# GpSimd's inverse square roots: a power in place of a seed and three Newton steps, in a two-layer decoder on one Trainium2 core

## The reference, cut to what matters

```
x = x + xattn0(layernorm(x), ctx, mask)   # 16 query heads, 8 key heads of 128
x = x + ffn0(layernorm(x))                # silu(gate) * up, weights rounded to float8
x = x + xattn1(layernorm(x), ctx)         # 16 heads of 128, q and k root-mean-square normalised
x = x + moe(layernorm(x))                 # 16 experts, the best 2 for each row
```

```
def _layernorm(x, axis=-1, eps=1e-05):
    return (x - mean(x)) / sqrt(var(x) + eps)

def rmsnorm(x, g, eps=1e-5):
    return x * rsqrt(mean(square(x)) + eps) * g
```

## Time and profile before

| | us |
|---|---|
| three runs, median | 2196.19 |
| three runs, lowest and highest | 2195.21, 2196.66 |
| the profiled execution, span | 2195.1 |
| TensorE busy | 2071.1 |
| VectorE busy | 1566.6 |
| ScalarE busy | 1253.3 |
| GpSimd busy | 574.9 |

### The profile page before, as it was taken

One profiled execution on the slowest core, in us unless ns is written; L12 is line 12 of the kernel. 1 busy time (PEld: TensorE's weight loads), 2 busy tenths in 40 slices (PEclk: granted clock), 3 DMA queues, 4 the chain that ended last, 5 costly groups with the idle time before them and its releaser, 6 DMA issues. The chain is left out here.

```text
span 2195.1 us, 36404 instructions
## 1 busy us (share of the span) xinstructions
PE 2071.1 (94%) x11594; PEld 1788.0 (81%) x11594; DVE 1566.6 (71%) x3714; ACT 1253.3 (57%) x3253; POOL 574.9 (26%) x1480
## 2 busy tenths in 40 slices
PE   5999999999999899999899999999999999599992
PEld 5888988888888778887788888888888887378882
DVE  6787677777779884444677777777777777767775
ACT  4555445455445533324776766677676666567771
POOL 2001001001001002223333434433343433145541
PEclk8999999999999999999999999999999999799996
DMA  7232122121211220002111111111111111278886
GB/s 249 82 99 89 63 85 92 62 89 63 90 63 49 73 77 1 1 1 77 49 58 49 62 63 57 48 57 48 57 62 72 48 40 39 87 269 290 290 275 257
DMA packets 78509, 202.10 MB, mean 92 GB/s; under 512 B 8689, under 2 KB 38409, under 8 KB 66209
## 3 DMA queue, kind: packets, MB, share of 16 engines
q1 hardware_dynamic: 68672, 179.37, 23.5%
q0 software_dynamic: 7520, 16.80, 2.2%
q10 hardware_dynamic: 2176, 4.19, 0.5%
HBM read 179.09 MB, written 29.10 MB: 95 GB/s over the span
## 5 line engine op out<-in xcount | busy, mean ns | idle before, releaser
L733 PE MATMUL bank<-l_wkv_hi,l_ctxT 128*128 128x512 f32 (+1 forms) x768 | 224.8, 364 | 9.0 <-PEq L79 6.9
L1245 DVE TENSOR_TENSOR l_pT_lo<-bank,l_pT_hi 128x512 fp32r<-128x512 f32 x256 | 175.2, 684 | 69.7 <-ACT l_pT_hi L1071 69.6
L1065 ACT ACTIVATE l_probs<-l_scored,l_nbias 128x256 f32<-128x256 f32 x256 | 128.4, 504 | 167.8 <-DVE l_nbias L1318 167.8
L733 PE MATMUL bank<-xnT_hi,l_wq_hi 128*128 128x512 f32 x512 | 208.7, 408 | 0.8 <-DVEq L1551 0.7
L733 PE MATMUL bank<-l_wo_hi,l_oT_hi 128*128 128x512 f32 x512 | 208.4, 407 | 0.7 <-DVE l_oT_lo L1245 0.7
L733 PE MATMUL bank<-l_wo_hi,l_oT_lo 128*128 128x512 f32 x512 | 200.6, 392 | 0.0
L733 PE MATMUL bank<-xnT_hi,l_wq_lo 128*128 128x512 f32 x512 | 200.3, 391 | 0.0
L733 PE MATMUL bank<-l_wo_lo,l_oT_hi 128*128 128x512 f32 x512 | 200.2, 391 | 0.0
L733 PE MATMUL bank<-xnT_lo,l_wq_hi 128*128 128x512 f32 x512 | 200.2, 391 | 0.0
L1071 ACT CAST l_pT_hi<-bank 128x512 fp32r<-128x512 f32 x256 | 150.8, 589 | 67.6 <-PE bank L832 67.6
L1333 DVE TENSOR_SCALAR l_probs<-l_probs,l_rden 128x256 f32<-128x256 f32 x512 | 181.3, 396 | 9.0
(11 more groups left out here) (305 smaller groups left out, 5738.0 us busy)
## 6 DMA issues: line engine op xcount, KB each, us to landing
l_ctxT<-ctx_split SPq DMA_DIRECT2D x63, 1024.0 KB, 4.8
moe_raw_gu<-in_L_ffn_gate_up_proj SPq DMA_DIRECT2D x31, 1024.0 KB
moe_raw_dn<-in_L_ffn_down_proj SPq DMA_DIRECT2D x31, 512.0 KB
l_raw_a<-in_L_xattn_Wq SPq DMA_DIRECT2D x16, 512.0 KB, 5.8
l_raw_a<-in_L_xattn_Wo SPq DMA_DIRECT2D x16, 512.0 KB, 5.6
x_sb<-in_x SPq DMA_DIRECT2D x4, 1024.0 KB, 9.1
l_v_next<-l_kn SPq DMA_DIRECT2D x16, 256.0 KB, 2.0
l_v_lo<-l_v_next SPq DMA_DIRECT2D x16, 256.0 KB, 2.6
```

Of the source, the lines that this page charges most:

```text
L733: mm = nc.tensor.matmul(out, a[x], b[y], start=(i == 0), stop=(i == n - 1))
L1065: ins = nc.scalar.activation(probs[u % 2][:, t, :], src, ACT.Exp, bias=nbias[:, i:i + 1], scale=scale, accum_out=rsum[:, i:i + 1])
L1245: nc.vector.tensor_tensor(pair[1], src, pair[0].bitcast(F32), ALU.subtract).then_inc(done, 1)
```

## The change

Every root on GpSimd becomes one instruction, `v ** -0.5`, a two-input operation whose second input is a small constant tensor of -0.5, written once at the start. The counts of the semaphores follow. VectorE's roots stay as they are.

```diff
+ROOT_STEPS = 1
+
+def root_of(gp, y, v, half, step):
+    step(gp.tensor_tensor(y, v, half[:, 0:v.shape[1]], ALU.pow))
...
             gp.memset(zero[:, :], 0.0).then_inc(ident_made, 1)
-            pool.wait_ge(ident_made, 1)
+            gp.memset(k.half[:, :], -0.5).then_inc(ident_made, 1)
+            pool.wait_ge(ident_made, 2)
...
-            pe.wait_ge(ident_made, 2)
+            pe.wait_ge(ident_made, 3)
...
-            sums, var, rr, tmp = (sb(n, [P, nk + nq]) for n in ("sums", "var", "rr", "tmp"))
+            sums, var, rr = (sb(n, [P, nk + nq]) for n in ("sums", "var", "rr"))
...
-            norm_steps = 1 + RSQRT_STEPS
+            norm_steps = 1 + ROOT_STEPS
...
-                rsqrt_steps(gp, rr[:, cols], tmp[:, cols], var[:, cols], step, lambda: apart(k, pool))
+                root_of(gp, rr[:, cols], var[:, cols], k.half, step)
...
-            ln_steps = RSQRT_STEPS + 3
+            ln_steps = ROOT_STEPS + 3
...
-                rsqrt_steps(gp, rstd, tmp, var, step, lambda: apart(k, pool))
+                root_of(gp, rstd, var, k.half, step)
...
-                dve.wait_ge(k_chain, 1 + RSQRT_STEPS)
+                dve.wait_ge(k_chain, 1 + ROOT_STEPS)
...
-                dve.wait_ge(den_chain, 1 + RSQRT_STEPS)
+                dve.wait_ge(den_chain, 1 + ROOT_STEPS)
...
+        k.half = st.enter_context(nc.sbuf_tensor("half", [P, NT], F32))
```

More of the change, by code:

```diff
@@ L666, in ln_group_factors @@
                 at = slice(tiles[0], tiles[-1] + 1)
-                mean, var, rstd, tmp, shift = k.ln_mv[:, at, 0], *(a[:, at] for a in (k.ln_var, k.ln_rstd, k.ln_tmp, k.ln_shift))
+                mean, var, rstd, shift = k.ln_mv[:, at, 0], *(a[:, at] for a in (k.ln_var, k.ln_rstd, k.ln_shift))
                 done = [ln_steps * factors_before[0]]
```

## The result

| kernel | median us | runs | lowest to highest |
|---|---|---|---|
| before | 2195.21 | 5 | 2194.02 to 2196.66 |
| after | 2203.38 | 5 | 2201.41 to 2204.86 |

The ratio is 1.0035, 95% interval 1.0024 to 1.0046: the changed kernel is slower, by 8.2 us, where 9.0 us of gain were forecast. The profiled execution after has a span of 2200.1 us.

A forecast was written before the change was run, and what follows sets the result against it. TensorE, busy 94% of the span, was taken to bound the kernel, so only its waits behind GpSimd's roots counted. Gains of 5.5 + 1.3 + 2.2 = 9.0 us from 2196.2 gave 2187.2 us, range 2180 to 2212.

The forecast's parts named there:

- (d): Hidden places, priced at nothing: the first keys' root, the last group's factors, and the memset of the exponents.
- only the edges gain: Rival, chance 0.20: in second-attention bodies VectorE's lag just moves the wait; 2192.7 us, with a power of 0.7 to 1.0.
- the hold: Rival, chance 0.16: a bias or multiplications of VectorE stand still until GpSimd's power ends, making the kernel slower.
- The cost of the power: One GpSimd power replacing the thirteen steps of 3.91 us: estimated at 0.35 us, range 0.2 to 3.9.
- very long power: Case, chance 0.10: a power over some 4.2 us would uncover two of the hidden roots.
- Step (a): Second-attention bodies: earlier key scalings leave the fourth multiplications alone, TensorE's waits shrink; gain 5.5 us, bounds 0 and 9.7.
- the wait turning up before the third transposition instead of the fourth: Sign of a wrong forecast: TensorE's wait in second-attention bodies moves to an earlier transposition of probabilities.
- a root over 0.9 us: Sign of a wrong forecast: a GpSimd root longer than this, where 0.3 to 0.5 us was expected.
- Step (b): The opening: a shorter root lets normalised rows, query copy and scores come earlier; gain 1.3 us, between 0 and 3.4.
- Step (c): End of the first attention: normalised rows start earlier, TensorE's clock partly stays up; gain 2.2 us, bounds 1 and 4.
- The late first use: Case, chance 0.04: the first power of all comes late, beside a gain in the second-attention bodies.

The follow-up runs named there:

- e2: The changed kernel with every address as before: the exponents take the place of a scratch tensor, VectorE's roots use another scratch; 2191.56 us.
- e4: e2 with the thirteen-step roots again for the key and query roots of the second attention, powers only in the layer norm; 2191.55 us.
- e7: e2 with a second, useless power ahead of each key root but the first, putting off the key scalings; 2184.23 us.
- e8: e2 with GpSimd waiting, after the first of four key scalings, for VectorE's third multiplications of the body; 2185.61 us.
- e9: The changed kernel with 192 more unused bytes per partition behind the exponents, so everything behind lies 256 bytes further up than before; 2192.25 us.
- e3: The kernel before with only an unused tensor of 128 bytes per partition where the changed kernel puts its exponents; 2204.00 us.
- e5: The kernel before with 64 unused bytes per partition ahead of x_sb, so xnT and the weights move up together; 2195.72 us.
- e6: The changed kernel with its exponents in 8 columns instead of 16, so everything behind moves by 32 bytes instead of 64; 2203.70 us.
- e1: The kernel before with only an unused tensor of 64 bytes per partition where the changed kernel puts its exponents; 2206.37 us.
- e10: e2 with GpSimd waiting for VectorE's third multiplications of the body before it begins the four key scalings; 2184.68 us.

## Why the prediction was wrong

**The missing term.** The step that turns the sign is in (d): the new exponents were priced at nothing, for their memset. Their memset (0.11 us, at 0.96 in the trace after, where TensorE first works at 12.7) is hidden, but their 64 bytes are not free. From e2 to the kernel after are 11.8 us (10.3 to 13.5, as above). The pitches give about as much: 1536 query products x 3.8 ns (235.2 to 239.0, without the group at half clock) = 5.8, 768 products of xnT and `ffn_w` x 5.7 ns = 4.4, 384 of `ffn_w` and `ffn_fz` x 2.8 ns (227.0 to 229.8) = 1.1, together 11.3. With the placement restored the time is 2191.6, near the rival "only the edges gain", 2192.7. That 2203.4 lies within the wide range of 2180 to 2212 is luck: the slower side was there for the hold, which did not occur (see below).

**The cost of the power**, taken as 0.35, is 1.64. My bounds of 0.2 and 3.9 held it; the choice by the nearest row, a plain two-input step, did not. The thirteen passes stood only in my estimate. The very long power of the chances, longer than the chain of 3.91, did not occur.

**Step (a)**, +5.5, is 0 (e2 against e4). The collision was read rightly: the scalings hold the multiplications, and that reaches TensorE. They start 1213.69 - 1211.10 = 2.6 us behind the start of ScalarE's last key copy (at 1211.10 in the kernel after), where 1.34 was forecast and 5.8 had been, and lie wholly over the third multiplications. The wait there is 0.31 us in every body, in place of 0.17 and 0.45. What failed is the step that the held third multiplications would still be done in time for TensorE. With a power of 1.64 us they take 1.43 us and end at 1214.22 + 1.43 = 1215.65, and TensorE's transposition starts at 1215.70, behind a wait. Whether one of 0.35 us would have been short enough no run shows. The prize was real: e7 takes 7.3 us from e2, the size of the waits summed in the prediction. The other bound, 9.7 from the table of waits, was read too high: two of its 21 waits, together 4.6 us, lie outside 1090 to 1831, and the 19 within are 5.1 us. The sign of what would show this, "the wait turning up before the third transposition instead of the fourth", is what the trace has, and a root over 0.9 us too.

**Step (b)**, +1.3 forecast: the scores come 1.5 us earlier behind the variance step (9.90 to 8.40, e2), as argued. By 65 us it is 2.8: from the variance step to the first output copy are 27.59 us before and 24.81 in e2. What (b) did not count goes with the clock: its mean from 48 to 54 us went from 0.59 to 1.00. e8 and e9 show it from the other side. With the same power the clock there is granted at half (0.50) from 45.3 to 48.7 us, and the stretch takes 25.5 us. The rest of the 3.4 at 62 us is chance: the variance step starts anywhere between 35.7 and 37.6 in the twelve traces, and e3, without a power, is 2.7 ahead at 62 us.

**Step (c)**, +2.2 forecast: it is 3.7 at 719 us, of which 1.2 are gone at 733, and 2.6 are left (e4). That VectorE is late next, as was forecast, shows at 719.71 in e4, where ScalarE waits 0.38 us for a bias; that it is the whole of the 1.2 is not shown.

**The hold** (0.16), that VectorE's bias stands still until the key power over it ends, was the larger part of the 0.25 for a slower kernel, and it is not what made the kernel slower. In the trace after, 31 biases of the second attention lie wholly under a power, and each took 0.16 us; the 7 that took 0.50 lie under GpSimd's blocks of 2.83 us (one under a row of 1.44), as in the earlier trace rows. The key scalings do hold VectorE (multiplications of 0.62 us take 1.43), and so do the blocks (0.16 becomes 0.50). The power does not, though it reads SBUF too: a bias takes 0.16 us under one of 1.64. So what the rows before show of these two does not carry over to the power. The upper end of the range, 2212, counted on such a hold by the power, 0.6 us in each of 30 bodies: no run shows one.

**The late first use** (0.04), that the first power of all comes late, did not occur: it takes 1.68 us, beside a mean of 1.64.

## What to carry to other kernels

When an edit adds or removes an on-chip tensor, count what it moves: look at the distance between the two operands of the commonest products before and after, and at their pitch, and separate the address change from the edit by an unused tensor of the same size. When a chain gets shorter, ask where the work behind it lands; here a later start of GpSimd's scalings, by a wait, was worth more than all the shortening (7.3 us against 5.4). And look first at stretches in which the changed instruction does not occur: here the steady loss there was that of the addresses.

## What the hardware showed that I had not expected

- The products of xnT with `l_wq` and with `ffn_w` run at 235 and 228 ns in the kernel before and in e2, e5 and e9, where the operands lie a multiple of 256 bytes apart in a partition, and at 238 to 240 and 233 with 32 (e6), 64 (after, e1) or 128 (e3) bytes more, about 2% slower, without a wait in the records. No run shows why, nor what other distances would do.
- The shift reaches products of `ffn_w` and `ffn_fz` whose own distance is unchanged. Their neighbours are not the reason: between products of their own kind, too, the pitch goes from 226.8 to 229.0 ns behind an `ffn_fz_hi` and to 231.2 behind an `ffn_fz_lo`. With all addresses moved together (e5) it stays at 227.0. And of the three kinds of product with `moe_w_gu`, two are not slowed. So the distance of a product's own operands does not explain all of it, and what does no run shows.
- A power on GpSimd of 128x8 takes 1.64 us, of 128x4 1.01, and does not hold VectorE: 31 pairs of multiplications under the power in e7 take 0.62 us, and 31 two-input biases in the kernel after 0.16, what they take alone.
- A bias of VectorE that GpSimd's scalings held was released about where the third of the four ends, not at the end of the row of four: the bias above ends at 1208.72, inside 1206.95 to 1209.28. The 24 biases of e10's second attention that start 1.15 or 1.16 us behind the scalings take 0.62 or 0.63 us. The six that start 1.08 or 1.09 us behind them take 0.16.
